# A cond-adapter and transformer block on one core: three groups of one-time work placed elsewhere in the first two chunks

## The reference

```python
hidden = gelu(x @ down_W.T + down_b)                            # 64 wide
hidden = hidden @ Wsel.T + bsel   (valid ids; else hidden)      # one of 16 experts for each sequence
x = ln(((hidden + emb) @ up_W.T + up_b) + x) * gamma + beta
scale, shift = split(silu(sin_emb(timestep)) @ W_ada + b_ada)
x = ln(x) * (1 + scale) + shift
q, k, v = x @ Wq + bq, x @ Wk + bk, x @ Wv + bv                 # 16 heads of 16
probs = softmax(where(mask, -inf, q k^T / 4 + attention_bias))  # bias: 8 x 16 x 512 x 512, float32
x = x + (probs v) @ Wo + bo
h = ln(x) * g2 + beta2
out = x + gelu2(h @ W1 + b1) @ W2 + b2                          # gelu2(y) = y * sigmoid(1.702 y)
```

## Time and profile before

| | |
|---|---|
| median of three runs | 926.67 us |
| profiled execution, its own time | 927.12 us |
| its span, first to last record | 925.3 us |
| busy: TensorE, its weight loads | 889.5 us (96%), 670.5 us |
| busy: VectorE, ScalarE, GpSimd | 700.2, 717.8, 709.5 us |
| bytes moved | 206.36 MB, mean 223 GB/s |
| granted clock of TensorE, mean | 0.996 of full speed |

### The profile page before, as it was taken

How to read it: one execution, slowest core, us unless ns; L and a number is a source line. 1 busy time by engine, 2 the same in 40 slices (tenths; PEclk the granted TensorE clock), 3 DMA queues, 4 the chain that set the end, 5 groups by cost and what they waited for, 6 DMA issues and landing times.

```text
span 925.3 us, 20972 instructions
## 1 busy us (share of the span) xinstructions
PE 889.5 (96%) x6566; PEld 670.5 (72%) x6566; DVE 700.2 (76%) x1891; ACT 717.8 (78%) x1703; POOL 709.5 (77%) x425
## 2 busy tenths in 40 slices
PE   8888889999999999999999999999999999999988
PEld 5655657777777777777777777777777777777766
DVE  5777877788687877878787877878687887675652
ACT  7767888778787878878797788878788787867651
POOL 3977978897697868987787877889687987876700
PEclk8999999999999999999999999999999999999999
DMA  8889699777977789676987679776997669765300
GB/s 253 273 272 273 206 274 286 216 220 216 294 217 224 215 235 304 212 222 208 264 264 229 206 229 277 230 219 202 262 264 220 206 201 278 218 202 180 125 2 23
DMA packets 147040, 206.36 MB, mean 223 GB/s; under 512 B 14250, under 2 KB 61675, under 8 KB 146931
## 3 DMA queue, kind: packets, MB, share of 16 engines
q1 hardware_dynamic: 145538, 203.71, 74.0%
q10 hardware_dynamic: 1392, 1.31, 0.4%
HBM read 183.98 MB, written 20.99 MB: 222 GB/s over the span
## 4 chain that ended last, share of the span: by engine, by line
PE 84%; DVE 4%; issue 4%; POOL 4%; ACT 2%; DMA 2%; SPq 1%; DVEq 0%; POOLq 0%; ACTq 0%
PE tp L1044 20%; PE pv L996 12%; PE la L958 12%; PE sc L1035 11%; PE lc L943 10%; PE lb L724 5%; PE lb L977 3%; POOL bias_s L563 3%; PE lb L740 2%; PE la L706 1%; PE lc L698 1%; DVE xm L1381 1%; DMA bias_s<-in_bias 1%; PE la L686 1%; PE lb L686 1%
## 5 line engine op out<-in xcount | busy, mean ns | idle before, releaser
L563 POOL TENSOR_TENSOR bias_s<-mask_f,bias_s 128x1024 f32<-128x1024 f32 x248 | 582.7, 2373 | 110.7 <-DMA bias_s<-in_bias 109.5
L1707 DVE CUSTOM_DVE_ANT_0 bias_s<-sc,bias_s 128x512 f32<-128x512 f32 x512 | 347.8, 684 | 162.3 <-PE sc L1035 155.7
L1272 ACT ACTIVATE bias_s<-bias_s,mx 128x512 f32<-128x512 f32 x512 | 371.2, 725 | 70.8 <-DVE mx L1707 68.7
L1044 PE MATMUL tp<-ident,bias_s 128*128 128x128 f32 x2048 | 308.2, 273 | 7.7 <-ACT pT L1278 3.3
L1044 PEld LDWEIGHTS tp<-ident,bias_s 128*128 128x128 f32 x2048 | 251.7, 141 | 85.4 <-issue 17.0
L1278 ACT COPY pT<-tp 128x512 f32<-128x512 f32 x335 | 195.3, 583 | 100.0 <-PE tp L1044 98.1
L1035 PE MATMUL sc<-stk,stq 128*128 128x512 bf16 x512 | 195.0, 381 | 6.5 <-DVE mx L1707 6.1
L958 PE MATMUL la<-w_s,act_s 128*128 128x256 f32 x496 | 124.3, 380 | 0.0
L996 PE MATMUL pv<-pT,v_all 128*32 128x256 f32 x2048 | 123.8, 382 | 0.0
L1714 DVE COPY pT<-tp 128x512 f32<-128x512 f32 x177 | 121.2, 685 | 1.9 <-PE tp L1044 1.8
L943 PE MATMUL lc<-hT,w_s 128*128 128x256 f32 x464 | 119.4, 380 | 2.5 <-ACT hT L1221 1.9
(11 more groups left out here) (237 smaller groups left out, 867.7 us busy)
## 6 DMA issues: line engine op xcount, KB each, us to landing
bias_s<-in_bias SPq DMA_DIRECT2D x256, 512.0 KB, 4.6
stq<-q_parts SPq DMA_DIRECT2D x126, 96.0 KB, 4.1
stk<-k_parts SPq DMA_DIRECT2D x124, 96.0 KB, 3.9
k_parts<-kb SPq DMA_DIRECT2D x32, 192.0 KB, 2.3
q_parts<-qb SPq DMA_DIRECT2D x31, 192.0 KB, 2.4
k_parts<-kb SPq DMA_DIRECT2D x32, 128.0 KB, 2.3
stq<-q_parts SPq DMA_DIRECT2D x63, 64.0 KB, 4.6
stk<-k_parts SPq DMA_DIRECT2D x62, 64.0 KB, 4.0
```

The costliest lines, as they stand in the source:

```text
L563: pool.tensor_tensor(tile, mask_f[:, :, :], tile, ALU.subtract).then_inc(s["masked"], 1)
L1044: last = pe.transpose(tp[n % 2][:, kt * P:(kt + 1) * P], bias_s[:, n // 2 % NB, n % 2, kt * P:(kt + 1) * P], ident[:, :])
L1272: act.activation(tile, tile, ACT.Exp, bias=mx[:, t:t + 1], scale=-1.0, accum_out=sums[:, j, head_of(hh):head_of(hh) + 1]).then_inc(s["prob ...
L1707: dve.tensor_tensor_reduce(out=tile, in0=sc[t % 2][:, :], in1=tile, scale=1.0, scalar=BIG, op0=ALU.add, op1=ALU.min, accum_out=mx[:, t:t + ...
```

## The change

Four things are placed elsewhere; what is computed stays the same.

- **Norm and stacks in round 0.** In round 0 alone VectorE's norm of chunk 2 takes slots 4.6 to 10.6 (`DVE_FIRST`) and not 1.6 to 10.6, behind the stacks' copies. On GpSimd the masks of head 6 go ahead of that norm's first inverse.
- **Values.** In round 0 those of chunk 1 come first (slots 4.0 and 5.0, bank lb, moved at 5.6) and those of chunk 0 second (6.0 and 6.6, moved at 7.3), in bank lc. The first queries wait for one move of values, not two.
- **Experts.** Turned at 9.6 (before 9.0), spread at 11.6 (10.3), folded at 13.3, 20.0 and 25.0 (11, 13, 15), copied at 15.6, 22.3 and 27.3 (12, 14, 16). `ew_t` (of sequences 2 to 7) and `up_w` lie in x2s and not in pT.
- **W1.** Sums at slots 9 and 15 of round 1 (before 18 and 19 of round 0), scaling at 16.0 and 19.6, correction at 20.3 and 22.0. W1's load goes from the head of the program to slot 14 of round 0, and W2's from there to slot 4 of round 1.

```diff
-EXPERTS_AT = dict(turn=9.0, spread=10.3, fold=(11.0, 13.0, 15.0), copy=(12.0, 14.0, 16.0))
+EXPERTS_AT = dict(turn=9.6, spread=11.6, fold=(13.3, 20.0, 25.0), copy=(15.6, 22.3, 27.3))
+DVE_FIRST = dict(x1=4.6, st0=5.0, mv0=5.3, n1=6.6, n2=8.0, st1=8.6, mv1=9.0, m1=9.6, m2=10.6)
-W1_AT = dict(sums=(18.0, 19.0), scale=(20.3, 21.3), lift=(22.0, 23.0))
+W1_AT = dict(sums=(9.0, 15.0), scale=(16.0, 19.6), lift=(20.3, 22.0))
...
+        ew_t = x2s[1][0:A + 1, 0:(B - 2) * (A + 1)].rearrange("p (b o) -> p b o", b=B - 2)
+        up_w = x2s[0][0:A + 1, 0:D]
...
         def v_bank(c):
-            return lb
+            return lc if c == 0 else lb
...
             def fold_late(k):
                 if k == 0:
                     pe.wait_ge(s["spread"], 1)
-                    pe.wait_ge(s["d_stack"], GH)
+                    pe.wait_ge(s["d_v"], 2)
...
                         if t == AT["q"][0]:
-                            pe.wait_ge(s["d_v"], c + 1)
+                            pe.wait_ge(s["d_v"], 1 if i == 0 else c + 1)
...
-                        values(0, int(t) - 4)
-                    late = (6.0, 6.6) if i == 0 else AT["v"]
...
+                        values(1, int(t) - 4)
+                    if i == 0 and t in (6.0, 6.6):
+                        if t == 6.0:
+                            pe.wait_ge(s["d_stack"], GH)
+                        values(0, (6.0, 6.6).index(t))
...
-                    if i == 0 and t in W1_AT["sums"]:
+                    if i == 1 and t in W1_AT["sums"]:
...
-                AT = DVE_AT
+                AT = dict(DVE_AT, **DVE_FIRST) if i == 0 else DVE_AT
```

More of the change, by code:

```diff
@@ L451, in _ @@
                 load_bias(n)
-            load("w1_in", [(w1_s[:, :, :], w1.rearrange("(c p) n -> p c n", p=P))])
             load_x(2)
@@ L492, in steps @@
                     if i == 0 and t == 14.0:
+                        load("w1_in", [(w1_s[:, :, :], w1.rearrange("(c p) n -> p c n", p=P))])
+                    if i == 1 and t == 4.0:
                         load("w2_in", [(w2_s[:, :, :], w2.rearrange("(c p) n -> p c n", p=P))])
@@ L620, in effective @@
                 if part == 1:
-                    pool.tensor_tensor(ew_t[0:A, b0:b1, A], ew_all[:, b0:b1, A], ew_all[:, b0:b1, A + 1], ALU.add
+                    pool.tensor_tensor(ew_t[0:A, b0 - 2:b1 - 2, A], ew_all[:, b0:b1, A], ew_all[:, b0:b1, A + 1], ALU.add
                                        ).then_inc(s["eff"], 1)
@@ L645, in _ @@
             effective(2, B, 1)
+            mask_half(6, 0)
+            mask_half(6, 1)
             inverse0(2)
-            for hh in range(6, NB):
-                for j in range(2):
-                    mask_half(hh, j)
+            mask_half(7, 0)
+            mask_half(7, 1)
             inverse1(2)
@@ L810, in fold_expert @@
             def fold_expert(b, bank, j):
-                return pe.matmul(bank[0:A + 1, j * D:(j + 1) * D], ew_t[:, b, :], up_w, start=True, stop=True)
+                return pe.matmul(bank[0:A + 1, j * D:(j + 1) * D], ew_t0[:, b, :] if b < 2 else ew_t[:, b - 2, :], up_w, start=True, stop=True)
             def keep_busy(times):
@@ L861, in norm_steps @@
                             pe.wait_ge(s["d_k"], 1)
-                        if i == 1:
+                        if i == 2:
                             pe.wait_ge(s["d_w1"], 2)
@@ L881, in norm_steps @@
                         pe.wait_ge(s["d_q"], 1)
-                    if i == 0 and t == 5.0:
-                        pe.wait_ge(s["a_stack"], GH)
                     if i == 0 and t in (4.0, 5.0):
@@ L887, in norm_steps @@
                             pe.wait_ge(s["a_stack"], 3)
-                        values(0, int(t) - 4)
-                    late = (6.0, 6.6) if i == 0 else AT["v"]
-                    if qv and t in late:
-                        if t == late[0]:
+                        else:
+                            pe.wait_ge(s["a_stack"], GH)
+                        values(1, int(t) - 4)
[3 more added lines that the diff above has]
+                        values(0, (6.0, 6.6).index(t))
+                    if qv and i > 0 and t in AT["v"]:
+                        if t == AT["v"][0]:
                             pe.wait_ge(s["a_xt1"], c + 1)
@@ L895, in norm_steps @@
                             wait(pe, s["a_hT"], i - 1)
-                        values(c, late.index(t))
+                        values(c, AT["v"].index(t))
                     if pre and t in AT["k"]:
@@ L1239, in steps @@
                         act.wait_ge(s["turned"], 1)
-                        act.copy(ew_t[0:A, 2:B, 0:A], pv[0:A, 2 * A:B * A].rearrange("p (b o) -> p b o", o=A)
+                        act.copy(ew_t[0:A, :, 0:A], pv[0:A, 2 * A:B * A].rearrange("p (b o) -> p b o", o=A)
                                  ).then_inc(s["spread"], 1)
@@ L1243, in steps @@
                         move_stack(*(("k", 2) if t == 2.3 else ("q", 3)))
-                    if i == 0 and t in W1_AT["scale"]:
+                    if i == 1 and t in W1_AT["scale"]:
                         ct = W1_AT["scale"].index(t)
@@ L1354, in effective @@
                                      badb, ALU.mult))
-                su(dve.tensor_tensor(ew_t[0:A, b0:b1, A], ew_all[:, b0:b1, A], ew_all[:, b0:b1, A + 1], ALU.add))
+                su(dve.tensor_tensor(ew_t0[0:A, b0:b1, A], ew_all[:, b0:b1, A], ew_all[:, b0:b1, A + 1], ALU.add))
                 dve.tensor_tensor(ew_fin[:, b0:b1, :], ew_fin[:, b0:b1, :], ew_all[:, b0:b1, 0:A], ALU.add
@@ L1511, in values @@
                 b = c // 2
-                dve.wait_ge(s["p_v"], c + 1)
+                dve.wait_ge(s["p_v"], c + 1 if c > 1 else 2 - c)
                 wait(dve, s["pv_done"], 2 * NG * (b - 1))
-                if c % 2 == 0 and b < 2:
+                if c in (1, 2):
                     dve.wait_ge(s["v_zero"], b + 1)
@@ L1524, in _ @@
             su(dve.memset(h2[A:A + 1, :], 1.0))
-            su(dve.memset(ew_t[A:A + 1, :, 0:A], 0.0))
-            su(dve.memset(ew_t[A:A + 1, :, A:A + 1], 1.0))
+            for part in (ew_t0, ew_t):
+                su(dve.memset(part[A:A + 1, :, 0:A], 0.0))
+                su(dve.memset(part[A:A + 1, :, A:A + 1], 1.0))
             dve.wait_ge(s["vec_in"], 64)
@@ L1606, in norm_steps @@
                         dve.wait_ge(s["v_w_in"], 48)
+                        values(1)
+                    if i == 0 and t == 7.3:
                         values(0)
-                    if qv and t == (7.3 if i == 0 else AT["v"]):
+                    if qv and i > 0 and t == AT["v"]:
                         values(c)
@@ L1688, in steps @@
                     norm_steps(t)
-                    if i == 0:
+                    if i == 1:
                         w1_steps(t)
```

5 lines of the change are left out of this document (2 added, 3 removed).

## The result

The changed kernel takes 922.32 us (median of 5, 920.73 to 923.41); the kernel before 926.67 (5 runs, 925.11 to 928.32). The ratio is 0.9947, with a 95% interval of 0.9933 to 0.9961: 4.9 us faster, 3.6 to 6.2. The profiled execution took 922.32 us, its span is 920.5: 4.8 less than before on both counts.

The account below looks back on a forecast made before the run. TensorE's stream in rounds 0 and 1 was taken as the bound, with no other engine full. Round 0 at -9.1 us and round 1 at +3.5 gave -5.6, so a median of 921.1 us, range 918.0 to 926.8.

Parts of the forecast that it names:

- Slots 2 to 14: Early round 0: shorter TensorE waits and the second fold leaving bring slot 14's score 4.0 us earlier, bounds 0 to 6.6.
- The 0.7 at slot 12: Round 0: VectorE, busy without a break to slot 11, costs TensorE about 0.7 us at slot 12.
- The step that names the norm in front of the stacks: Early round 0: VectorE's norm of chunk 2 ahead of the stacks makes TensorE late; a 1.14 us wait at 45.77.
- Slots 15 to 31: Rest of round 0: sums leave and folds move, so the round ends 9.1 us earlier in all, bounds 5.2 to 12.
- The waits of 1.0 at slots 20 to 22: Late round 0: VectorE and ScalarE now set the pace, adding 1.0 us of new waits.
- What could hold that: Round 0: GpSimd's masks or DMA might limit the 9.1 us gain; mask margin of 2 to 4 us holds, thinly.
- The DMA bound of 49.5 us: Round 0: if its transfer rate is all there is, it cannot go below 49.5 us, a gain of 6.8.
- Round 1: W1's sums cost 1.3 us at slot 9 and 2.2 at 15, scaling and lift nothing: +3.5, bounds +1 to +10.1.
- A: Late round 0: masks come late, the round gains only 6.8 us, total 923.4 us; chance 0.15.
- B: Round 1, slots 9 to 22: all W1 work lands on the path, 10.1 us, total 930.0 us; chance 0.10.
- C: Early round 0: VectorE's find chain takes back the 4.0 us, total 926.7 us; chance 0.10.
- D: Round 1: idle TensorE time hides the sums but for 1 us, total 918.6 us; chance 0.15.

Follow-up runs that it names:

- e7: The changed kernel with the second half of W1's sums at slot 17 of round 1 and the first scaling at 18.6: 921.80 us.
- e5: The changed kernel with VectorE's norm of chunk 2 back at the slots of before (1.6 to 10.6): 924.00 us.
- e6: The changed kernel with the values as before: chunk 0 first, both in bank lb, first queries waiting for two moves: 923.53 us.
- e2: The changed kernel with W1's and the experts' slots and the loads of before, leaving norm and values changed: 924.30 us.
- e3: The changed kernel with the experts' turn, spread, folds and copies at the slots of before: 924.45 us.
- e8: The changed kernel with the experts' turn at 9.0 and spread at 10.3, folds left late: 922.48 us.
- e1: The kernel before with the W1 part of the change alone, including the loads of W1 and W2: 928.26 against 927.21 us.
- e11: The changed kernel without the four products with W1 in the sums, only to price them: 921.24 us.
- e4: The changed kernel with W1 scaled at slots 18.6 and 20.6 and lifted at 21.3 and 23.3 of round 1: 924.19 us.
- e12: The kernel of e10 with VectorE's norm of chunk 2 back at the slots of before: 920.74 us.
- e9: The kernel of e8 with the load of W1 at slot 26 of round 0 instead of 14: 919.89 us.
- e10: The kernel of e9 with the second half of the sums at slot 17 and the first scaling at 18.6: 919.03 us.

## Why the prediction was right, point by point

The forecast was 921.1 us with 918.0 to 926.8; it came to 922.32, 4.35 us below the kernel before where 5.6 were forecast. By the rounds: round 0 8.8 shorter, round 1 5.4 longer, round 2 1.35 shorter, together 4.7.

*Slots 2 to 14.* 4.0 predicted; from slot 0 to slot 14 it took 24.21 us (before 27.97): 3.8. The waits came as said: 0.66 at the stack (0.65), none for the values, 1.38 for the spread (1.5). The 0.7 at slot 12 isn't there; 0.92 stand at slot 8, which I had charged with nothing (bounds 0 to 1.2). In e7, the same instructions, it is the other way round, as predicted: none at slot 8, 0.57 at slot 12, and slot 14 after 23.81 us. Which of the two stands there depends on when the loads land. The step that names the norm in front of the stacks as what made TensorE late is wrong in size: it is worth 0.5 us at slot 5 and 0.1 to 0.5 at the end of the round (e5). The values are the larger part, 1.4 to 1.8 (e6).

*Slots 15 to 31.* 9.1 predicted at the start of round 1, 8.6 measured (8.8 from slot 0). The waits of 1.0 at slots 20 to 22 are there as 0.41 at slot 20 and smaller ones behind. W1's part is 5.2 us on top of norm and values (e2, e3), where I counted 5.16 of sums and 0.9 of hold-ups; the folds' 1.4 makes the rest.

*What could hold that.* Masks of head 8 on at 59.26 (58.9 predicted), a margin of 3.3 us for head 15 (2 to 4). Both right, and e8 shows how thin it was. The DMA bound of 49.5 us for round 0 took 14.8 MB at 263 / 0.88 = 299 GB/s. As a mean the rate was about right: the changed kernel's round 0 ran at 296 GB/s with the engines busy for 0.99. The bytes were not: 296 GB/s for 47.6 us are 14.1 MB, so 0.7 MB slid out of the round, and the margin of the masks went from 8.6 to 3.3 us with it. That is the exception which the prediction made. In shorter stretches the rate goes higher, here in the changed kernel:

```profile
70.00:80.00 10.00, 8.93 (x79) 5.96 (x79) 8.42 (x23) 8.51 (x24) 8.79 (x4) 1.00 1.07 348
75.00:80.00 5.00, 4.23 (x29) 3.04 (x28) 4.74 (x14) 5.00 (x15) 3.79 (x2) 1.00 1.06 396
```

And in the kernel before, while its first loads run:

```profile
15.00:30.00 15.00, 14.28 (x51) 8.30 (x50) 10.29 (x33) 8.79 (x21) 11.61 (x15) 0.77 1.05 384
```

So a mean rate divided by the busy share isn't what can be reached: 384 GB/s were held for 15 us. The Trainium skill's limit of about 358 GB/s per core (DMA: Bandwidth & Descriptors, section Bandwidth), which the prediction named, is not borne out either: 384 and 396 are above it.

*Round 1.* +3.5 predicted, +5.4 measured. From slot 8 to 14 it took 11.63 us where there were 10.20, so 1.4 (1.3 predicted for the first half). In e1 the sums alone cost this; in the changed kernel the wait of 1.03 us for the inverse, which I had not foreseen, stands beside them and would cost as much without their products with W1 (e11). The second cost 5.84 from slot 14 to 16 where there were 2.61, so 3.2 (2.2 predicted): this is the mis-sized term. It is 2.6 of products, with nothing hidden, and 0.65 of waiting, since the wait for the copy out of bank la is 0.82 us where 0.17 stood. Scaling and lift cost nothing at their slots, as said (the changed kernel was 4.65 us behind by slot 16, and e5, at full clock, is 4.67 behind at the end of the round); e4 shows that they cost 1.6 us a slot or two later (55.15 for 53.55 us). The last 0.7 is mostly the fall of the clock: e3, e5, e6 and e7 have round 1 at 53.55 to 53.64 without one. And one term was missing with the other sign: round 2 is 1.35 shorter. In the kernel before it held these two waits of TensorE, neither of which is in the changed kernel's round 2 or in round 3 of either; the third row, of VectorE, stands before them:

```profile
157.63 0.39 PE L1035 MATMUL sc<-stk,stq 128*128 128x512 bf16 x1 [0.46 <-DVE mx L1707]
...
162.00 0.63 PE L1044 MATMUL tp<-ident,bias_s 128*128 128x128 f32 x4 [0.85 <-ACT pT L1278]
...
155.29 0.88 DVE L1381 SCALAR_TENSOR_TENSOR la<-la,rs,beta_r 128x256 f32<-128x256 f32 x2 [1.80 <-POOL rs L582]
```

VectorE waited 1.80 us there for a norm's inverse, which stands behind the masks in GpSimd's stream. The length of round 2 goes with this wait from kernel to kernel: 1.80 us and a round of 54.31 before, 1.56 and 54.36 in e2, 1.28 and 53.99 in e1, 0.42 and 53.32 in e3, none and 53.05 in e5, none and 52.96 in the changed kernel. So the 1.35 us go with GpSimd's stream, which is earlier against TensorE's, and not with W1's place alone (e1 gave back 0.3); that this stream is the cause is argued, since no run moved it alone. At full clock rounds 1 and 2 together grew by 106.60 - 103.19 = 3.4 us (e5). That my 3.5 matches this is luck: one error in round 1 and one in round 2 cancel.

*Rivals.* A did not happen in the changed kernel in round 0 and does one microsecond further (e8); its beginning is the wait of 1.03 us in round 1. B: round 1 stayed under 58 us, and not all of the products was on the path (e11). C: slot 14 came at 61.08, and e2 kept all of its early gain in the profiled execution. D was too hopeful: round 1 has idle time, but not where the sums stand.

*Open.* By rounds, the changed kernel is 1.2 us ahead of e3 (1.7 for e5, at full clock), by the ratios 3.1. The ends of the two intervals are 0.5 us apart, so the smaller figure is possible; falls of the clock in the runs without a profile could be the rest, and can't be seen. How much the norm's place is worth is open too (e5, e12).

## What to carry to other kernels

Work moved out of a full stage into a looser one costs what its own place has no gap for: here all of the second half of the sums, and of the first half about half (e1). Taken alone it gained nothing. It went with folds that stand later, in the bank that the sums left free, and those gained 1.2 us by the rounds (e3); whether late folds would have paid with the sums in their old place was not tried. When a stage gets shorter, the transfers and the masks that it holds do not: the executions with a round 0 under 46.5 us (e8, e9, e12) all took 54.5 us or more for round 1 (53.4 in e10), waiting for a mask and an inverse. Look for what can be loaded outside of such a stage before taking out the next microsecond (e8 gained nothing; with W1's load and the sums moved as well, e10 gained 2.8 us). Where two waits in a row guard the same later point, as the stack's copy and the landing of the keys here, removing the first alone is worth what the second leaves.

## What the runs showed of the hardware

The granted clock of TensorE fell to its lower level for some 3.4 us in rounds 0 and 1. In the rows before each fall the engine had a wait of 1.3 to 1.4 us and was little busy (0.93 of 2 us in the changed kernel, 2.13 of 4 in e4, 2.65 of 4 in e11, 2.79 of 4 in e1). It doesn't follow from the instructions alone: at one place of the same stream it fell in one execution and not in another (round 0 in e4 and e11 and not in the changed kernel, nor in e7, with the same waits as e4 and TensorE busy for 2.37 of 4 us; slot 20 of round 1 in the changed kernel and e1, and not in e3 to e6). The Trainium skill says of a kernel's start that where the clock changes varies from run to run (TensorE: Matmul & The Clock Gate, Part 1). In the middle of one, the runs here show that even whether it changes varies. A fall cost 1.2 to 1.6 us in round 0 (48.85 in e4 and e11 against 47.63 and 47.23) and 0.7 in round 1. There the changed kernel was 1.7 us behind e5 at slot 22 and 0.8 at slot 24, so part of it was made up in waits that shrank. In the first 37 us it fell in every profiled execution, for 3 to 10 us. Such falls are as large as most effects tried here, so a kernel of this size is compared by stages with the clock beside them.
